# Cross-attention with gated fusion on one core: where GpSimd's row-sum additions start, and the order of VectorE's softmax list

## What is computed

```python
mp     = mem @ W_mem.T                       # 1601 x 512
attn   = softmax(x @ mp.T / sqrt(512))       # 512 x 1601
c      = attn @ mp
gate   = sigmoid([x, c] @ W_gate.T + b_gate)
fused  = x + gate * c
out    = fused * rsqrt(mean(fused**2) + 1e-6) * norm_w
```

## Time and profile before

| What | Value |
|---|---|
| median of three runs | 579.77 us |
| the profiled execution, its own time | 579.95 us |
| its span in the profile | 577.8 us |
| TensorE busy | 542.7 us, 94% |
| VectorE busy | 485.7 us, 84% |
| ScalarE busy | 313.6 us, 54% |
| GpSimd busy | 165.3 us, 29% |
| mean granted TensorE clock | 0.994 |

### The profile page before, as it was taken

How to read it: one execution, slowest core, us unless ns; L and a number is a source line. 1 busy time by engine, 2 the same in 40 slices (tenths; PEclk the granted TensorE clock), 3 DMA queues, 4 the chain that set the end, 5 groups by cost and what they waited for, 6 DMA issues and landing times.

```text
span 577.8 us, 8830 instructions
## 1 busy us (share of the span) xinstructions
PE 542.7 (94%) x2432; PEld 437.5 (76%) x2432; DVE 485.7 (84%) x760; ACT 313.6 (54%) x599; POOL 165.3 (29%) x128
## 2 busy tenths in 40 slices
PE   8898899989999899998999899998999989998994
PEld 6775788868788678877788687886788867887883
DVE  4766958899698996899878997889969899689946
ACT  4666626476364735567364773647546573556713
POOL 0005500057003550046200580015600364004741
PEclk9999899999999999999999999999999999999998
DMA  9864173502655028621485115650265403201033
GB/s 217 251 128 75 36 131 89 102 19 75 137 125 110 0 82 163 138 63 29 126 154 101 35 36 152 139 100 18 73 150 129 93 13 103 84 24 36 2 110 109
DMA packets 184337, 54.25 MB, mean 94 GB/s; under 512 B 161528, under 2 KB 174848, under 8 KB 184320
## 3 DMA queue, kind: packets, MB, share of 16 engines
q1 hardware_dynamic: 183792, 53.52, 40.5%
q10 hardware_dynamic: 528, 0.52, 0.3%
HBM read 45.63 MB, written 8.39 MB: 93 GB/s over the span
## 4 chain that ended last, share of the span: by engine, by line
PE 75%; DVE 13%; issue 4%; SPq 4%; DMA 2%; ACT 1%; DVEq 0%; ACTq 0%
PE bank L344 17%; PE bank L346 16%; PE bank L345 16%; PE bank L511 8%; PE bank L512 8%; PE bank L513 8%; DVE fused L933 5%; DVE p_lo L790 3%; DVE fused L923 2%; DMA fused<-in_L_xattn_W_gate_dram 2%; SPq L241 2%; SPq L233 1%; PE bank L531 1%; PE bank L446 1%; DVE gate L849 1%
## 5 line engine op out<-in xcount | busy, mean ns | idle before, releaser
L1118 POOL TENSOR_TENSOR psum_rows<-psum_rows,p_tmp 128x512 f32<-128x512 f32 (+1 forms) x88 | 136.7, 1553 | 63.0 <-ACT p_tmp L660 60.8
L1118 POOL TENSOR_TENSOR psum_rows<-p_tmp 128x512 f32<-128x512 f32 x8 | 10.4, 1300 | 327.6 <-ACT p_tmp L660 327.6
L660 ACT ACTIVATE p_tmp<-s 128x512 f32<-128x512 f32 (+1 forms) x104 | 65.5, 630 | 69.9 <-DVE s L831 67.6
L344 PE MATMUL bank<-q_hi,mt_hi 128*128 128x512 f32 (+1 forms) x208 | 81.7, 393 | 0.0
L345 PE MATMUL bank<-q_lo,mt_hi 128*128 128x512 f32 (+1 forms) x208 | 81.2, 390 | 0.0
L346 PE MATMUL bank<-q_hi,mt_lo 128*128 128x512 f32 (+1 forms) x208 | 81.1, 390 | 0.0
L512 PE MATMUL bank<-p_lo,mem_hi 128*128 128x512 f32 (+1 forms) x208 | 81.0, 389 | 0.0
L511 PE MATMUL bank<-p_hi,mem_hi 128*128 128x512 f32 (+1 forms) x208 | 81.0, 389 | 0.0
L513 PE MATMUL bank<-p_hi,mem_lo 128*128 128x512 f32 (+1 forms) x208 | 80.9, 389 | 0.0
L790 DVE TENSOR_TENSOR p_lo<-p_tmp,p_hi 128x512 fp32r<-128x512 f32 (+1 forms) x104 | 80.2, 772 | 0.0
L622 ACT ACTIVATE s<-bank 128x512 f32<-128x512 f32 (+1 forms) x104 | 62.0, 596 | 19.6 <-PE bank L346 19.2
(11 more groups left out here) (92 smaller groups left out, 1033.8 us busy)
## 6 DMA issues: line engine op xcount, KB each, us to landing
mem_raw<-in_ctx_dram SPq DMA_DIRECT2D x48, 256.0 KB, 2.7
mem_blocks<-in_ctx_dram SPq DMA_DIRECT2D x64, 136.0 KB
x_again<-in_x_dram SPq DMA_DIRECT2D x32, 256.0 KB, 2.7
out_dram<-fused SPq DMA_DIRECT2D x32, 256.0 KB, 2.1
x_raw<-in_x_dram SPq DMA_DIRECT2D x112, 64.0 KB, 2.0
mem_blocks<-in_ctx_dram SPq DMA_DIRECT2D x56, 64.0 KB, 2.0
x_raw<-in_x_dram SPq DMA_DIRECT2D x4, 256.0 KB, 5.1
gate<-in_L_xattn_W_gate_dram SPq DMA_DIRECT2D x2, 512.0 KB, 5.9
```

Source lines behind the costliest of these rows:

```text
L344: nc.tensor.matmul(dst, a_hi, b_hi, start=(start and i == 0), stop=False)
L660: nc.scalar.activation(p_tmp[0:r, t % TMP_RING, :], s[0:r, t, :], ACT.Exp, scale=float(D) ** -0.5).then_inc(exp_done, 1)
L1118: nc.gpsimd.tensor_tensor(psum_rows[0:r, :], a, p_tmp[0:r, t % TMP_RING, :], ALU.add).then_inc(p_added, 1)
```

## The change

Three edits. In `add_p`, GpSimd waits for `p_has_lo` of the tile in place of `exp_done`. In ScalarE's list the four `xt_hi_part` stand one place earlier. VectorE's list for the softmax part is reordered: the `gate_ctx` operations and `shift` stand in another order, `add_bias` stands further up, `p_lo_part(0)` behind `add_x(2)` and `p_lo_part(1)` behind `add_x(3)`, and `mem_lo_part(4)` and `mem_lo_part(5)` stand ahead of the `p_lo_part` they stood behind.

```diff
-        TANH_AT, SQUARES_AT, NEXT_X_AT = {0: 1, 2: 2, 3: 3}, {3: 0, 4: 1, 5: 2, 7: 3}, {9: 0, 10: 1, 11: 2, 12: 3}
+        TANH_AT, SQUARES_AT, NEXT_X_AT = {0: 1, 2: 2, 3: 3}, {3: 0, 4: 1, 5: 2, 7: 3}, {8: 0, 9: 1, 10: 2, 11: 3}
@@ VectorE, iteration
                     shift(b, 2)
+                    shift(b, 3)
+                    p_lo_part(b, 0)
+                    weights(V[1])
+                    shift(b, 4)
+                    add_bias(b, 0, first)
                 else:
...
                     shift(b, 0)
                     shift(b, 1)
-                    shift(b, 2)
                     gate_ctx(b - 1, 1)
                     gate_input(b - 1, 2)
                     add_x(b - 1, 1)
-                shift(b, 3)
-                p_lo_part(b, 0)
-                if first:
-                    weights(V[1])
-                else:
+                    shift(b, 2)
                     gate_ctx(b - 1, 2)
                     gate_input(b - 1, 3)
                     add_x(b - 1, 2)
-                shift(b, 4)
+                    p_lo_part(b, 0)
+                    shift(b, 3)
+                    gate_ctx(b - 1, 3)
+                    add_bias(b, 0, first)
+                    add_x(b - 1, 3)
+                    shift(b, 4)
                 p_lo_part(b, 1)
-                if not first:
-                    gate_ctx(b - 1, 3)
                 shift(b, 5)
+                add_bias(b, 1, first)
                 p_lo_part(b, 2)
-                if not first:
-                    add_x(b - 1, 3)
-                add_bias(b, 0, first)
                 shift(b, 6)
-                p_lo_part(b, 3)
                 if not last:
                     transpose_x(b + 1, 0, first)
+                p_lo_part(b, 3)
                 shift(b, 7)
-                add_bias(b, 1, first)
+                add_bias(b, 2, first)
                 p_lo_part(b, 4)
+                shift(b, 8)
                 if not last:
                     transpose_x(b + 1, 1, first)
-                shift(b, 8)
+                mem_lo_part(b, 4)
                 p_lo_part(b, 5)
-                add_bias(b, 2, first)
                 shift(b, 9)
+                add_bias(b, 3, first)
                 p_lo_part(b, 6)
-                mem_lo_part(b, 4)
                 shift(b, 10)
-                add_bias(b, 3, first)
-                p_lo_part(b, 7)
-                mem_lo_part(b, 5)
-                shift(b, 11)
-                p_lo_part(b, 8)
                 if not last:
                     xt_lo_part(b + 1, 0)
                     transpose_x(b + 1, 2, first)
-                shift(b, 12)
-                p_lo_part(b, 9)
-                mem_lo_part(b, 6)
+                mem_lo_part(b, 5)
+                p_lo_part(b, 7)
+                shift(b, 11)
                 if not last:
                     xt_lo_part(b + 1, 1)
                     transpose_x(b + 1, 3, first)
-                p_lo_part(b, 10)
+                p_lo_part(b, 8)
+                shift(b, 12)
+                mem_lo_part(b, 6)
+                p_lo_part(b, 9)
                 if not last:
                     xt_lo_part(b + 1, 2)
                     transpose_mem(b + 1, 0, first)
-                p_lo_part(b, 11)
+                p_lo_part(b, 10)
                 if not last:
                     xt_lo_part(b + 1, 3)
                     transpose_mem(b + 1, 1, first)
+                p_lo_part(b, 11)
                 p_lo_part(b, 12)
@@ GpSimd, add_p
-                pool.wait_ge(exp_done, MT * b + t + 1)
+                pool.wait_ge(p_has_lo, MT * b + t + 1)
```

## The result

| | Median, us | Runs | Span of the profiled execution |
|---|---|---|---|
| before | 579.56 | 578.68 to 580.42 | 577.8 |
| after | 598.31 | 597.19 to 598.81 | 595.8 |

The changed kernel is slower: its time is 1.0321 of the time before (95% interval 1.0299 to 1.0343). The forecast was 589.3, the range 580 to 595. The direction was right, the size was half of what came.

The account below looks back on a forecast made before the run. The prediction took TensorE, waiting about 3.4 us of a 68.3 us batch for VectorE's list, as the bound. Batch 0 -1.8, loop +6.6, batch 7 -0.4 and end +5.1 made +9.5: 589.3 us, range 580 to 595.

Parts of the forecast that it names:

- The bound and the start of the softmax: TensorE waits about 3.4 us per batch for VectorE; new order idles VectorE 4.4 us, yet gate_x(2) gains 1.1 us.
- batch 0: First batch: add_bias(1) no longer stands behind a transpose_x waiting for x, so the query comes earlier: -1.8 us.
- the hand-over taken as 0.08: VectorE's p_lo to GpSimd's addition in the softmax: 0.08 us, from the one such hand-over in the trace.
- My bound: Hand-over to GpSimd and back, once per tile: 0.1 us more costs each batch another 0.6 us, +4 in all.
- `mem_lo_part(6)` and what stands behind it: VectorE's list late in the softmax: tile 8's low part at 346.8, tile 9's at 349.0, fourth xt_lo_part about 351.4.
- -0.4 for batch 7: Last batch: gate_x(2) gives 1.1 us, tile 9 costs some 0.4; -0.4 us taken as low parts run closer.
- +5.1 at the end: Last row sums start 5.1 us late, waiting for additions 11 and 12 behind the outputs; what follows is as before.
- the row of 7.21 us: Earlier trace's addition, started at 545.97, kept out by unbroken VectorE operations until output ended; taken as the order of service.
- The row sums 3.4 us late: Alternative end by the Trainium skill: additions and outputs alternate, row sums start 3.4 us late, sum 0.9 us lower.
- the u parts as the last to arrive: In the alternating alternative at the end, the u parts behind the outputs would be last.
- a rival: Break-even in the loop: contention saved covers the new idle time, total 583 us; chance 0.17.
- The rival "faster": VectorE's run from shift(4) to the fourth xt_lo_part needs 2 us less than stepped: total 571.5 us; chance 0.15.

Follow-up runs that it names:

- both kernels with the short list: Kernel before with the new wait, add_bias(0) and (1) further up, last two xt_lo_part ahead of transpose_mem: 555.88 us; also with batch 7's additions behind exp: 550.91 us.

## Why the prediction came out right in direction and half in size

**The bound and the start of the softmax: right to 0.1 us.** `gate_ctx(1)` starts at 322.95 here, 4.54 us behind the 318.41 of the earlier trace rows. Shifted by that, my steps give 332.84 for `add_bias(0)`, 333.59 for gate_x(2), 335.44 for the end of `p_lo(1)` and 339.54 for the first weighted tile. The trace has 332.85, 333.59, 335.38 and 339.54. The idle times ahead of `gate_ctx` are 1.74 us where I had 1.8, `exp(4)` is released by GpSimd as said, and batch 0 gives 1.9 us where I had 1.8. This last agreement is luck in part: in another execution of the same instructions, told above, it is 3.8.

**The first step that failed: 1.9 us from one addition to the next, the hand-over taken as 0.08.** It is 2.0, and GpSimd's timeline shows it:

```profile
335.47 1.29 POOL L1118 TENSOR_TENSOR psum_rows<-p_tmp 128x512 f32<-128x512 f32 x1 [40.74 <-DVE p_lo L790]
337.48 1.30 POOL L1118 TENSOR_TENSOR psum_rows<-psum_rows,p_tmp 128x512 f32<-128x512 f32 x1 [0.71 <-DVE p_lo L790]
339.49 1.30 POOL L1118 TENSOR_TENSOR psum_rows<-psum_rows,p_tmp 128x512 f32<-128x512 f32 x1 [0.71 <-DVE p_lo L790]
```

An addition of 1.30 us; the `p_lo` under it (336.51 + 0.80 = 337.31) ends 0.55 us behind it; and 0.17 us later the next addition starts. That makes 2.02. Only the first addition of the batch comes 0.09 us behind its `p_lo`, as in the row that I had read in the tail. All later ones of this batch come 0.15 to 0.17 behind, also where the `p_lo` itself was not held up, as at 343.26 + 0.68 = 343.94:

```profile
343.26 0.68 DVE L790 TENSOR_TENSOR p_lo<-p_tmp,p_hi 128x512 fp32r<-128x512 f32 x1
344.10 1.30 POOL L1118 TENSOR_TENSOR psum_rows<-psum_rows,p_tmp 128x512 f32<-128x512 f32 x1 [1.31 <-DVE p_lo L790]
```

Why the first one is quicker no run here shows. My bound ("0.1 us more, each batch loses another 0.6") named the right term. 0.5 of its 0.6 us had come by tile 6, whose low part ends at 345.94 where my steps, shifted, give 345.44. By tile 8 half of it was made up again by steps that I had taken too long (351.61 against 351.34).

**The second: `mem_lo_part(6)` and what stands behind it, priced too short.** My steps have 2.2 us from the low part of tile 8 to that of tile 9 (346.8 to 349.0); with `mem_lo_part(6)` meeting addition 8 and taking 1.54 us it is 2.66. From there to the end of the fourth `xt_lo_part` it is 2.6 where I had 2.4, and the query starts 0.13 behind that end where I had it start at once. So the query starts at 357.00 instead of 355.94: 0.27 us from the additions up to tile 8, 0.46 from `mem_lo_part(6)`, 0.2 from the last steps and 0.13 from the hand-over to TensorE. This 1.1 us more per batch, six times, is 6.5 of the missing 8.5 us. How these waits fall was as forecast: tile 8 (0.98), tile 9 (0.94), query (1.02).

**The third: -0.4 for batch 7.** It is +0.9. gate_x(2) gave the 1.1 us (its start-to-start step went from 2.67 to 1.58), but tiles 8 and 9 together come 1.4 late, start to start, where I had 0.4 for tile 9. That gives +0.3; of the remaining 0.6, some 0.3 stands at gate_x(3) (548.00), which had no gap before, and 0.2 in the second matmuls behind the waits.

**The fourth: +5.1 at the end, all of it a wait, then "what follows is as before".** The row sums start 3.33 us late, not 5.1 (573.55 against the last matmul's step from 569.99 to 570.22), and what follows takes 2.6 us more, because its first 5 us or so run at the lower clock (granted 0.50 from 573.4 to 579.0 above, the 1.2 GHz level) after the wait. The two errors nearly cancel, 5.95 against 5.1. I had let the unbroken outputs keep additions 11 and 12 out by the row of 7.21 us. VectorE's and GpSimd's rows at the end of the kernel after say otherwise:

```profile
568.93 5.77 DVE L943 SCALAR_TENSOR_TENSOR fused<-fused,r_rms,norm_rows 128x512 f32<-128x512 f32 x4 [1.47 <-POOL r_rms L1127]
```

```profile
568.87 4.63 POOL L1118 TENSOR_TENSOR psum_rows<-psum_rows,p_tmp 128x512 f32<-128x512 f32 x3
```

Three additions ended at 573.50 with four outputs stretched to 5.77 us from 2.73: they took turns. By the Trainium skill, "SBUF — State Buffer", section "Who interferes with whom", the order of issue decides who blocks the other; here the addition started 0.06 us ahead of the first output, and the trace agrees. The row sums 3.4 us late, which the prediction worked out by that page, are what came (3.3); the u parts as the last to arrive, its other half, did not: TensorE has no wait for them in the profile of this kernel.

The other order of service is in the same trace, in five of the six loop batches. An addition that started under a `p_lo` was kept out until the four outputs, unstretched, were over:

```profile
357.68 4.78 POOL L1118 TENSOR_TENSOR psum_rows<-psum_rows,p_tmp 128x512 f32<-128x512 f32 x1
358.59 2.71 DVE L943 SCALAR_TENSOR_TENSOR fused<-fused,r_rms,norm_rows 128x512 f32<-128x512 f32 x4
```

In the sixth loop batch the addition (217.78) again started 0.06 us ahead of the first output (217.84), and the output took 1.77 us. The addition of the earlier trace rows started, at 545.97, while a `p_lo` was running (545.36 to 546.04), and was kept out. So these rows sort by which engine was at work first; no run changes that alone. The same section of the Trainium skill has the shared ports held for one instruction, where these additions were kept out for a whole run of instructions; there the measurement decides.

Together: 6.5 + 1.3 + 0.85, less 0.1 in batch 0, is the 8.5 us between +9.5 and +18.0.

**What I had missed altogether is the size of what the change was after.** I wrote that two hits on `add_x` cost 1.4 us per batch, and used it only as an argument for a rival. The experiment with the wait alone shows that these, the hits on `mem_lo_part(6)` and TensorE's wait at gate_x(2) go together, and are worth 17 us. One line of the diff is the best single edit of those run here, and the rest of it undoes that gain twice over. The rival "faster" named the right place, the run from `shift(4)` to the fourth `xt_lo_part`; its 2 us per batch came off only in kernels that, unlike the changed one, have no `tanh` waits.

## What to carry to other kernels

Where an in-order engine hands work to another and later needs its answer, count what the list has between the two: `gate_ctx(j)` right behind the `shift` that ScalarE must first turn into exp, p_hi and tanh costs 1.74 us each time, while the five or six operations that stood between them before left no such wait. Split a change of several edits into a table of each alone and both: here one edit was worth -17 us, the other +9, and the pair +18. A VectorE operation with two tensors in SBUF must be priced by what GpSimd runs beside its new place, not by its duration in the old one: the same `mem_lo_part(6)` took from 406 to 1396 ns in the mean of these kernels.

## What the runs showed of the hardware that was not expected

- **The clock after a wait.** TensorE's idle times of 2.1 to 2.5 us were followed by half speed in some batches and not in others of the same execution: at the query 5 of 7 times with the memory splits behind p_lo, 4 of 7 with `add_bias` up and the old wait, never at the seven waits of 2.3 to 2.4 us at gate_x(2) in the kernel before. Each time it costs about 1.5 us (68.7 against 67.1, 68.8 against 67.3). The length of the wait alone does not decide it. With `add_bias` up the longest, 3.00 us, was followed by full speed (query at 75.06, next matmul at 75.39, then steps of 0.23), while 1.81 us ahead of batch 1's query in both kernels with the short list, and 1.03 and 0.76 us close together at the end of the first of them, were followed by matmuls at 0.43 us. What decides it stays open.
- **Waits of about 1 us in the loop kept the clock.** In the kernel after none of the loop's waits of about 1 us was followed by matmuls at 0.43 us; with the waits gathered in one of 2.2 us at the query the list's gain was given back.
- **Who yields.** A `p_lo` under an addition ended 0.55 us behind it, the small memory tile 0.29 (351.77 + 1.61 = 353.38, and 352.13 + 1.54 = 353.67). The duration in the profile holds its waiting, so 65x256 took 406 ns alone and 1540 ns beside an addition.
